# A hybrid block on one core: the output gate of its gated linear attentions made by blocks of 512 tokens, and their lead-in put in another order over one ring of seven PSUM banks

## What is computed

```python
q1 = (x @ Wq).reshape(B, L, H, DK) * scale;  k1 = (x @ Wk).reshape(...);  v = (x @ Wv).reshape(...)
q2 = (x @ Wqa @ Wqb).reshape(...) * scale;   k2 = softmax((x @ Wka @ Wkb).reshape(...), axis=-1)
gk1 = log_sigmoid(x @ Wg1a @ Wg1b + bg1) / 16        # decay of the dense part
gk2 = log_sigmoid(x @ Wg2a @ Wg2b + bg2) / 16        # decay of the four experts' part
mask, rw = top_1_of(softmax(x @ We))
# S_t = diag(exp(gk_t)) S_{t-1} + k_t^T v_t ;  o_t = q_t S_t   for the dense part and each expert
o = gla(q1, k1, v, gk1) + sum_e gla(q2 * rw_e, k2 * rw_e, v, gk2 * mask_e)
g = (x @ Wga @ Wgb).reshape(B, L, H, DV)              # the output gate
o = o * rsqrt(mean(o * o) + EPS) * norm_w * (g * sigmoid(g))
return o @ Wo
```

## Time and profile before

| | |
|---|---|
| median of 3 runs | 3519.05 us (3514.82 to 3520.2) |
| the profiled execution | 3517.08 us, its span 3515.8 us |
| busy | PE 3060.8 us (87%), DVE 2660.0 (76%), ACT 2029.9 (58%), POOL 948.3 (27%) |
| mean granted TensorE clock | 0.902 |
| first gated linear attention | 676.4 to 1148.2 us |
| second | 1819.6 to 2291.5 us |

### The profile page before, as it was taken

The page is one execution under the profiler, slowest core; times in us unless marked ns, Lnnn a source line. Parts: engine busy times, 40 slices in busy tenths (PEclk is TensorE's granted clock), DMA queues, the critical chain, the costliest instruction groups (busy, mean ns, idle before and its releaser), DMA issues. The chain is left out here.

```text
span 3515.8 us, 59236 instructions
## 1 busy us (share of the span) xinstructions
PE 3060.8 (87%) x23828; PEld 1443.7 (41%) x23828; DVE 2660.0 (76%) x3307; ACT 2029.9 (58%) x3741; POOL 948.3 (27%) x977
## 2 busy tenths in 40 slices
PE   6999999789999699999978999955566887999879
PEld 1222222356666222222235666621223543667745
DVE  8999999546655799999954565579896556787544
ACT  4999999544544499999954454443332234444022
POOL 0000000233333000000013333336775420676400
PEclk7999999879999699999987999977888887999779
DMA  2000000000000100000000000000000000000000
GB/s 89 14 16 15 15 15 15 8 1 1 1 1 1 55 13 16 15 15 14 15 11 1 1 1 1 1 23 0 0 0 9 1 1 0 1 1 1 1 0 13
DMA packets 30221, 35.43 MB, mean 10 GB/s; under 512 B 13623, under 2 KB 24058, under 8 KB 29690
## 3 DMA queue, kind: packets, MB, share of 16 engines
q1 hardware_dynamic: 29754, 31.57, 3.1%
q10 hardware_dynamic: 192, 0.07, 0.0%
HBM read 19.16 MB, written 7.34 MB: 8 GB/s over the span
## 5 line engine op out<-in xcount | busy, mean ns | idle before, releaser
L418 DVE TENSOR_REDUCE max_parts<-banks 128x2 f32<-128x1024 f32 x1024 | 1168.8, 1215 | 18.9 <-PE banks L306 18.8
L508 ACT ACTIVATE probs<-banks 128x512 f32<-128x512 f32 x2048 | 1082.2, 599 | 73.9 <-PE banks L313 57.1
L306 PE MATMUL banks<-k_parts,q_parts 48*128 48x512 bf16 x2048 | 621.9, 396 | 48.6 <-DMA k_parts<-k_scratch 24.4
L313 PE MATMUL banks<-q_parts,k_parts 51*128 51x512 bf16 x2048 | 654.8, 386 | 6.6
L331 PE MATMUL banks<-probs,v_heads 128*9 128x256 f32 x8192 | 637.8, 383 | 7.5 <-ACT pv_copy L519 0.3
L313 PEld LDWEIGHTS banks<-q_parts,k_parts 51*128 51x128 bf16 x2048 | 148.0, 94 | 482.9 <-ACT probs L508 418.1
L548 POOL CAST neg_max_parts<-neg_max 128x8 bf16<-128x8 f32 x64 | 13.0, 203 | 1150.9 <-DVE neg_max L423 1150.9
L331 PEld LDWEIGHTS banks<-probs,v_heads 128*9 128x9 f32 x8192 | 123.7, 88 | 378.9 <-issue 340.2
L1444 PE MATMUL banks<-decay,ident 128*128 128x512 f32 x256 | 153.4, 746 | 107.2 <-POOL decay L1410 107.2
L1410 POOL TENSOR_TENSOR decay<-state,c_row 128x1024 f32<-128x1024 f32 x64 | 212.2, 3337 | 77.5 <-DVE state L1473 77.5
L1473 DVE TENSOR_TENSOR_SCAN state<-decay,state_carry,state 128x1024 f32<-128x1024 f32 x64 | 210.0, 3319 | 0.0
(11 more groups left out here) (429 smaller groups left out, 5491.7 us busy)
## 6 DMA issues: line engine op xcount, KB each, us to landing
outT_half<-pv_copy SPq DMA_DIRECT2D x252, 16.0 KB
prob_sums<-pv_copy SPq DMA_DIRECT2D x252, 2.0 KB
q_scratch<-qk_parts SPq DMA_DIRECT2D x8, 384.0 KB, 3.9
k_scratch<-qk_parts SPq DMA_DIRECT2D x8, 384.0 KB, 2.6
k_parts<-k_scratch SPq DMA_DIRECT2D x32, 96.0 KB
q_parts<-q_scratch SPq DMA_DIRECT2D x28, 96.0 KB
k_parts<-k_scratch SPq DMA_DIRECT2D x32, 64.0 KB
q_parts<-neg_max_rows SPq DMA_DIRECT2D x128, 3.0 KB
```

The lines of the kernel that those rows point to most:

```text
L306: nc.tensor.matmul(Mb[m % 2][:, blk(x)], Q[p % 2][half_of(x, ROWS), tile(t)], K[p % 2][half_of(x, ROWS), blk(b)], start=True, stop=True).t ...
L313: nc.tensor.matmul(bank("exp", n, x)[:, :], K[p % 2][half_of(x, ROWS + PARTS), tile(t)], Q[p % 2][half_of(x, ROWS + PARTS), blk(j)], start ...
L418: nc.vector.tensor_reduce(mxp[s % 2][:, :, u // NB, u % NB], Mb[m % 2].rearrange("p (x k) -> p x k", x=2), AX.X, ALU.max).then_inc(*maxed. ...
L508: nc.scalar.activation(PT[:, n % RING, x, :], bank("exp", n, x)[:, :], ACT.Exp, scale=float(HD) ** -0.5).then_inc(*exped.inc())
```

## The change

Four things, all in `gla_ffn` and its ring:

- **The output gate by blocks.** One `gate_project(i)` now makes one quarter of the features for a block of 512 tokens (one matmul of 64 rows by 512 columns) instead of all features of one tile of 128. Block 0's four stand in the lead-in, the others in steps 0 to 11 (i = t+4); steps 12 to 14 have none. In the loop it writes Dbank, after `mask_queries` has read it, and `update_dense` waits for `weigh_gate`. The buffer `sg` is one of 512 columns, and `sigmoid(i)` waits for `weigh_gate(i-1)` as before.
- **Between the gate groups.** In a step, PE does the first decay gate, then the output gate, then the second decay gate. `weigh_gate` moves on DVE from behind `dense_queries` to behind `finish_gates`. The use `gp` is gone from the ring of three.
- **One ring of seven banks in the lead-in** instead of three and four; the loop's ring of three starts where it ends.
- **The lead-in's order.** Tile 0's steps stand ahead of the low-rank work of the next blocks, on PE, ACT and DVE; all four layer-norm applications are on DVE; POOL's memsets wait until the first of them is done.

The core of the diff:

```diff
     def before(self, u, t):
 
         i = self.at[u, t] - len(self.banks)
-        return self.read_out(i) if i >= 0 else (self.read_out(0)[0], 0)
...
-FIRST_USES = "v klow q2 cum0 cum1 half g0 g1 gp k1 q1 tk0 tq0 tk1 tq1".split()
-TILE_USES = "cum0 cum1 v klow q2 half g0 g1 gp k1 q1 rs tk0 tq0 tk1 tq1 out".split()
+TILE_USES = "cum0 cum1 v klow q2 half g0 g1 k1 q1 rs tk0 tq0 tk1 tq1 out".split()
 USES_AHEAD = dict(rs=0, out=0, g0=2, g1=2)
 MASK_TURNS, SAME_EXPERTS = 0, 1
+ENTRY_USES = (("turned", 0), ("glow", 0), ("low", 0), ("g0", 0), ("g1", 0), ("v", 0), ("klow", 0), ("q2", 0), ("mask", 0), ("turned", 1), ("glow", 1), ("low", 1),
+              ("same", 0), ("cum0", 0), ("cum1", 0), ("k1", 0), ("q1", 0), ("half", 0), ("tk1", 0), ("tq1", 0), ("turned", 2), ("glow", 2), ("low", 2),
+              ("g0", 1), ("gp", 0), ("g1", 1), ("tk0", 0), ("tq0", 0), ("gp", 1), ("gp", 2), ("gp", 3), ("turned", 3), ("glow", 3), ("low", 3))
...
-        gate, sg = two("out_gateT", [128, 4, 128]), sb("gate_sigmoid", [128, 4, 128])
+        gate, sg = two("out_gateT", [128, 4, 512]), sb("gate_sigmoid", [128, 512])
...
-        norm = LayerNorm(g, mem, None, pool_from=1)
+        norm = LayerNorm(g, mem, None)
...
+        entry = Ring(g.ps[0:7], ENTRY_USES, readers)
+        ring = Ring(g.ps[0:3], uses, readers, entry)
         norm.banks = [entry.bank("turned", b) for b in range(NB)]
-        bank, bank_read = ring.bank, ring.before
+        part = lambda u, t: entry if (u, t) in entry.at else ring
+        bank, bank_read = lambda u, t: part(u, t).bank(u, t), lambda u, t: part(u, t).before(u, t)
+        gate_bank = lambda i: entry.bank("gp", i) if i < NB else Dbank
...
-            def gate_project(t):
-                pe.wait_ge(*bank_read("gp", t))
+            def gate_project(i):
+                b, r = i // 4, i % 4
+                pe.wait_ge(gates_copied, b + 1)
+                if i < NB:
+                    pe.wait_ge(*entry.before("gp", i))
+                else:
+                    pe.wait_ge(q_masked, i - NB + 1)
+                nc.tensor.matmul(gate_bank(i)[:, :], w["Wc"][0:64, tile(r)], a2T[0:64, blk(b)], start=True, stop=True).then_inc(*gate_projected.inc())
+
+            def gate_logit(t, k):
+                u, r = f"g{k}", 64 + 32 * k
                 pe.wait_ge(gates_copied, t // 4 + 1)
-                for r in range(4):
-                    i = nc.tensor.matmul(bank("gp", t)[:, tile(r)], w["Wc"][0:64, tile(r)], a2T[0:64, tile(t)], start=True, stop=True)
-                i.then_inc(*gate_projected.inc())
-
-            def gates(t):
-                pe.wait_ge(gates_copied, t // 4 + 1)
-                for k, r in ((0, 64), (1, 96)):
-                    u = f"g{k}"
-                    pe.wait_ge(*bank_read(u, t))
-                    nc.tensor.matmul(bank(u, t)[:, :], a2T[r:r + 17, tile(t)], w["Wc"][r:r + 17, :], start=True, stop=True).then_inc(*gate_logits.inc())
+                pe.wait_ge(*bank_read(u, t))
+                nc.tensor.matmul(bank(u, t)[:, :], a2T[r:r + 17, tile(t)], w["Wc"][r:r + 17, :], start=True, stop=True).then_inc(*gate_logits.inc())
 
...
             def update_dense(t):
                 pe.wait_ge(q_masked, t + 1)
+                pe.wait_ge(gate_made, min(t + 1 + NB, NT))
...
+            gate_logit(0, 0)
+            gate_logit(0, 1)
+            values(0)
+            low_keys(0)
+            low_queries(0)
+            turn_mask(entry, 0)
             turn(1)
-            gates(0)
-            values(0)
             low_gates(1)
             low_rank(1)
             route(1)
-            turn_mask(entry, 0)
-            low_keys(0)
-            low_queries(0)
             same_expert(entry, 0)
             cumulate(0)
+            keys(0)
+            queries(0)
+            halves(0)
+            turn_k1(0)
+            turn_q1(0)
             turn(2)
             low_gates(2)
             low_rank(2)
             route(2)
-            halves(0)
-            gates(1)
+            gate_logit(1, 0)
             gate_project(0)
-            keys(0)
-            queries(0)
+            gate_logit(1, 1)
+            turn_k0(0)
+            turn_q0(0)
+            gate_project(1)
+            gate_project(2)
+            gate_project(3)
             turn(3)
             low_gates(3)
             low_rank(3)
             route(3)
-            turn_k0(0)
-            turn_q0(0)
-            turn_k1(0)
-            turn_q1(0)
             for t in range(NT):
                 after = t + 1 < NT
                 scores(t, 0)
...
                 if t + 2 < NT:
-                    gates(t + 2)
-                if after:
-                    gate_project(t + 1)
+                    gate_logit(t + 2, 0)
+                if t + NB < NT:
+                    gate_project(t + NB)
+                if t + 2 < NT:
+                    gate_logit(t + 2, 1)
...
-            def weigh_gate(t):
-                dve.wait_ge(gate_sigmoid, t + 1)
-                dve.wait_ge(gated, t - 1)
-                nc.vector.scalar_tensor_tensor(flat(gate[t % 2]), bank("gp", t)[:, :], w["norm"], flat(sg), ALU.mult, ALU.mult).then_inc(*gate_made.inc())
+            def weigh_gate(i):
+                b, r = i // 4, i % 4
+                dve.wait_ge(gate_sigmoid, i + 1)
+                dve.wait_ge(gated, 4 * (b - 1))
+                nc.vector.scalar_tensor_tensor(gate[b % 2][:, r, :], gate_bank(i)[:, :], w["norm"], sg[:, :], ALU.mult, ALU.mult).then_inc(*gate_made.inc())
...
+            norm.apply(1)
+            choose_experts(0, first)
             norm.statistics(2)
-            choose_experts(0, first)
             finish_gates(0)
             subtract_max(0)
             mask_same(entry, 0)
+            norm.apply(2)
             norm.statistics(3)
             normalise_keys(0)
             expert_queries(0)
-            finish_gates(1)
             decay_keys(0)
             dense_queries(0)
-            weigh_gate(0)
+            norm.apply(3)
+            finish_gates(1)
+            for i in range(NB):
+                weigh_gate(i)
             dve.wait_ge(zeroed, 2)
             highest_logit(1, others)
...
+                if t + NB < NT:
+                    weigh_gate(t + NB)
                 add_state(t, 0)
                 add_state(t, 1)
                 if after:
                     decay_keys(t + 1)
                     dense_queries(t + 1)
-                    weigh_gate(t + 1)
...
             norm.deviation(0)
-            norm.deviation(1)
             norm.copy(0)
             copy_low_gates(0)
             exp_logits(0, first)
             copy_low_rank(0)
-            norm.deviation(2)
-            norm.copy(1)
+            norm.deviation(1)
             softplus(0)
             copy_values(0)
             keep_queries(0)
+            copy_mask(entry, 0)
+            exp_keys(0)
+            norm.deviation(2)
+            norm.copy(1)
             copy_low_gates(1)
-            copy_mask(entry, 0)
             copy_low_rank(1)
-            exp_keys(0)
-            norm.deviation(3)
             exp_cumulated(0)
+            act.wait_ge(zeroed, 1)
+            exp_half(0)
+            copy_k1T(0)
+            copy_q1T(0)
             norm.copy(2)
             copy_low_gates(2)
             copy_low_rank(2)
-            act.wait_ge(zeroed, 1)
-            exp_half(0)
+            norm.deviation(3)
             softplus(1)
-            sigmoid(0)
+            copy_k0T(0)
+            copy_q0T(0)
+            for i in range(NB):
+                sigmoid(i)
             norm.copy(3)
             copy_low_gates(3)
             copy_low_rank(3)
-            copy_k0T(0)
-            copy_q0T(0)
-            copy_k1T(0)
-            copy_q1T(0)
             for t in range(NT):
                 after = t + 1 < NT
                 if after:
```

63 lines of the change are left out of this document (32 added, 31 removed).

## The result

The changed kernel takes **3522.64 us** (median of 20 runs, 3519.78 to 3524.51), the kernel before 3515.78 us in the same session (20 runs, 3511.97 to 3527.37). The ratio is 1.0015, with a 95% interval of 1.0008 to 1.0022: 7 us slower by the medians, which is inside the 0.2% that I had called no change. I had forecast 3552. The time lies in my range, but the likeliest case, slower by 0.9%, was not what happened.

The account below looks back on a forecast made before the run. It took PE to bound the loop and a chain of short waits at the slow clock the lead-in. Twice (11.7 lead-in + 5.0 loop + 0.3) = +34 us gave 3552 us, main case 3535 to 3570, full range 3500 to 3572.

Parts of the forecast that it names:

- no change: Whole kernel: outcome "same", within some 0.2% (7 us) of the kernel before; given 10%.
- lead-in: Before the loop: first scores 11.7 us later in each linear attention, with four sigmoids instead of one; bounds +8 and +15.
- steps 2 to 11: Loop's ten steps: 27.1 us each with a long clock fall, 271 us against 259.3 and 262.5.
- steps 12 to 14: Loop's end, without output gate: 22.8 us a step on average, 68.4 us against 75.1 and 71.9.
- The clock in the loop: Steps 2 to 11: the granted clock falls in every step, each a long fall costing 3.2 us.
- the 0.1 of new waits: Loop step: PE waits 0 to 0.3 us at the turns of decayed keys and queries, taken as 0.1.
- The hole (1): Loop: PE's wait ahead of `sum_squares`, for the bank of `gp`, goes; gain 1.53 us a step.
- the serial gates (2): Steps 0 to 11: gate matmuls of 17, 64, 17 rows run one after another, 3.18 us for 2.14; loss 1.04.
- Side by side gates: Rival, loop: all three gate matmuls run at once in 1.06 us instead of 2.14, giving 3456 us; 9%.
- A lead-in that isn't longer: Rival, lead-in: the seven-bank ring lets sigmoids hide behind block 3's work, giving 3521 to 3527 us; 8%.
- The clock doesn't fall in every step, or only briefly: Rival, loop: short falls give 3512 us, none gives 3478; 16%.
- my main case: Whole kernel: longer lead-in and a long clock fall in every step 2 to 11, 3552 us, 0.9% slower; 60%.

Follow-up runs that it names:

- e3: Kernel before with only the output gate's matmuls moved from the ring of three to Dbank from tile 1 on: 3465.41 us, ratio to before 0.9840.
- e1: Changed kernel with the loop's output gate behind the two decay gate groups (17, 17, then 64 rows) instead of between them: 3476.89 us, ratio to before 0.9873.
- e4: Changed kernel with the output gate of blocks 1 to 3 contracting 32 of 64 rows, so half the sum is missing: 3440.90 us, ratio to before 0.9766.
- e7: e1 with `halves` placed behind `intra` instead of right ahead of the gates: 3602.20 us, ratio to before 1.024.
- e10: e6 with `halves` placed behind the values' matmul: 3534.26 us, ratio to before 1.0061.
- e6: e5 with two sigmoid buffers in the lead-in and tile 1's two gate groups side by side there: 3457.16 us, ratio to before 0.9834.
- e8: e6 with `intra` placed between `halves` and the gates, ring order kept: 3453.09 us, ratio to before 0.9817.
- e9: e6 with `halves` placed ahead of the values' matmul: 3503.36 us, ratio to before 0.9963.
- e5: Changed kernel with the edits of e1 and e2 together: 3461.02 us, ratio to before 0.9844.
- e2: Changed kernel with block 3's copies placed between the lead-in's sigmoids on ACT instead of behind all four: 3517.78 us, ratio to before 0.9992.

## Why the prediction was wrong, point by point

Set against the windows of the first attention, the prediction's terms came out so:

| term | predicted, us | measured, us |
|---|---|---|
| lead-in | +11.7 | +7.9 |
| steps 0 and 1 | 0 | +1.8 |
| steps 2 to 11 | +11.7 (271 for 259.3) | +3.8 |
| steps 12 to 14 | -6.7 | -10.3 |
| together | +17 | +3.2 |

**The step that failed** is "The clock in the loop": "I take a fall in every one of steps 2 to 11, and of the long kind". The fall in every step came; the kind didn't. Three of ten falls were of the short kind (3 x 1.6 = 4.9 us less), and a step with a long fall took 26.8 us and not 27.1, since the hole is 1.70 us by the starts and not 1.53 and the 0.1 of new waits didn't come: 3.0 us less over ten steps. Together that is the 7.9 us of the table. Why three falls were short stays open. In steps 12 to 14 I had 68.4 us and 64.4 came: I gave each two thirds of a short fall and the profile has one in all (1.6 us less), steps 12 and 13 are shorter for the same two reasons (21.5 at full clock for 21.7), and I had overlooked that step 14 is shorter by itself (19.9 us at full clock); it has no decay gates to make. (The table has 3.6 us there and not 4.0, as the steps of the kernel before take 74.7 us when cut at L906 and 75.1 in the earlier trace rows.)

**The hole (1) and the serial gates (2)** were right, and both are shown: e3 takes the hole away alone, e1 and e4 the serial matmuls by two different means. What e1 adds is that the serial gates cost more than their 1.05 us: with the clock they were worth 45.7 us over 24 steps. My forecast had that too, as long falls in every step, and put it too high.

**The lead-in** was right in its mechanism (the four sigmoids 2.8 us apart, 2.7 forecast, with block 3's copy behind them) and wrong in one duration: I had the log of tile 1 end at 726.3, and it ended at 722.56. From `cumulate(0)` to tile 1's first gate I had 15.2 us (704.3 to 719.5), with the durations of the kernel before, and it took 12.0 (703.39 to 715.42), most of it at the full clock with PE busy for 9.62 of 10.4 us. Windows view of the changed kernel, from the keys to the first gate matmuls, and behind it:

```profile
706.90:717.30 10.40, 9.62 (x49) 6.08 (x47) 4.06 (x9) 5.12 (x11) 0.00 (x0) 0.99 0.00 0
717.30:737.80 20.50, 14.35 (x26) 6.08 (x26) 4.29 (x6) 12.16 (x19) 0.00 (x0) 0.50 0.00 0
```

The log's 3.7 us are the 3.8 us of the table. The second lead-in, at 63.9 us for 55.5, was 8.4 us longer.

**Steps 0 and 1** I had left as they are, with a bound of 2 us; +1.8. That is a sum of larger terms: two holes are gone (-3.4), the gates are serial (+2.0), and the time at the low clock by the rows above is 24 us for 17 (+3.3 at 1.6 for 3.4).

**The rivals.** Side by side gates (9%): excluded by the trace. A lead-in that isn't longer (8%): excluded. "The clock doesn't fall in every step, or only briefly" (16%): half of it was true, three brief falls. The measured time lay between my main case and this rival, and closest to "no change", to which I had given 10%. The excluded rival of a lead-in that isn't longer gives 3521 to 3527, which holds the measured 3522.64 by luck. Large terms of either sign (hole -51, steps 12 to 14 without the gate's matmuls -6, serial gates with their clock +46, and +18 that remain for the lead-ins and what follows them) came within 7 us of each other; the sum's own error of some 15 us per attention should have given "same" more than that.

## What to carry to other kernels

A matmul of 64 rows between two of 17 rows costs more than its place: keep matmuls of one tile height together, so that those on distinct rows run side by side, and put the other behind. Here this one exchange of two lines turned a change that was 0.15% slower into one 1.3% faster. Equal height isn't enough if the second of a pair waits for its bank (e7, e10). Where a loop has PE busy throughout, count what an edit does to the granted clock as a term of its own, and take the two kinds of fall from the rows before saying which will come. A long-lived bank in a ring is a wait for whoever comes three uses later, so look first for a bank outside the ring (e3: 1.6%).

## What the runs showed that I had not expected

- The clock's falls depend on the order of the same matmuls: e6, e8 and e9 do the same work in a step without a new bank wait, and their steps 2 to 11 spend 39, 19 and 67 us at the low clock. Neither the unbroken length of nearly empty work nor its being close together explains all three. (e7 and e10, with 91 and 68 us, have a wait that parts a pair.)
- The clock can carry an edit's effect into steps that it doesn't touch: steps 0 and 1 take 61.6 us at 0.83 in e1 and 57.1 at 0.91 in e5, which differ in the lead-in only, with the same idle time. In e2 the same edit did much less.
- Of all runs e8 is the fastest that computes the whole: 3453.09 us, ratio to before 0.9817 (0.9804 to 0.9831), 2% faster than the changed kernel.
